# A shorter input ring, ten more groups of the spectrum kept on chip, and a new order of transfers between two stages

## The reference

```python
coeff = complex(xi[..., 0], xi[..., 1]) * sqrt_eig
x = einsum('nlm,mlk->nkm', coeff, pct)           # Legendre sums, one product per order m
u = irfft(x, n=512, axis=-1, norm='forward')     # h: 64 x 256 x 512
h = u + attention(layernorm(u))                  # key = x K, tanh logits, band of 12, softmax
h = h + ffn(layernorm(h))                        # 7 layers, only rows that a mask selects
```

## Time and profile before

| what | us |
|---|---|
| median of three runs (range) | 1428.83 (1427.85 to 1432.66) |
| the profiled execution, its own time | 1430.64 |
| span of its trace | 1428.6 |
| last group of stage 1 scaled | 319.05 |
| SyncE's first issue of stage 2 | 325.27 |

### The profile page before, as it was taken

One profiled execution on the slowest core, in us unless ns is written; L12 is line 12 of the kernel. 1 busy time (PEld: TensorE's weight loads), 2 busy tenths in 40 slices (PEclk: granted clock), 3 DMA queues, 4 the chain that ended last, 5 costly groups with the idle time before them and its releaser, 6 DMA issues. The chain is left out here.

```text
span 1428.6 us, 30500 instructions
## 1 busy us (share of the span) xinstructions
PE 1334.1 (93%) x8813; PEld 1158.9 (81%) x8813; DVE 929.4 (65%) x2026; ACT 899.9 (63%) x1956; POOL 559.5 (39%) x1394
## 2 busy tenths in 40 slices
PE   4999778798999999999999999999999989999994
PEld 3778666588899999999999999999999989545551
DVE  1232222235777878878788887888878878767772
ACT  1223222234677777777777777777777777867772
POOL 0000000000355555555555555555555546732222
PEclk8999999999999999999999999999999999999997
DMA  8999999994653433434334343343434332100000
GB/s 346 424 425 424 425 425 425 425 376 146 192 130 92 94 79 96 86 83 90 79 98 85 82 86 82 99 83 83 85 82 100 82 93 59 50 12 9 9 4 5
DMA packets 88315, 219.69 MB, mean 154 GB/s; under 512 B 20784, under 2 KB 33724, under 8 KB 75900
## 3 DMA queue, kind: packets, MB, share of 16 engines
q1 hardware_dynamic: 78728, 190.33, 42.8%
q10 hardware_dynamic: 4164, 27.27, 4.5%
q0 software_dynamic: 5376, 1.52, 0.6%
HBM read 147.77 MB, written 72.68 MB: 154 GB/s over the span
## 5 line engine op out<-in xcount | busy, mean ns | idle before, releaser
L674 PE MATMUL ps_k<-sphi,Glo 128*128 128x256 f32 x1024 | 292.2, 285 | 0.0
L673 PE MATMUL ps_k<-splo,Ghi 128*128 128x256 f32 x1024 | 291.0, 284 | 0.0
L672 PE MATMUL ps_k<-sphi,Ghi 128*128 128x256 f32 x1024 | 288.6, 282 | 0.0
L261 PE MATMUL s1b<-pg,cg 128*128 128x256 f32 x1024 | 240.5, 393 | 48.0 <-DVE cg L231 46.8
L261 PEld LDWEIGHTS s1b<-pg,cg 128*128 128x128 f32 x1024 | 198.0, 196 | 93.0 <-issue 33.9
L231 DVE TENSOR_TENSOR cg<-xg,se 128x1024 f32<-128x1024 f32 x63 | 77.2, 1225 | 221.5 <-DMA pg<-in_pct_dram 211.0
L1442 POOL TENSOR_SCALAR ve<-var 128x2 f32<-128x2 f32 x64 | 13.9, 217 | 479.8 <-ACT squares L1049 479.7
L672 PEld LDWEIGHTS ps_k<-sphi,Ghi 128*128 128x128 f32 x1024 | 194.7, 190 | 2.4
L673 PEld LDWEIGHTS ps_k<-splo,Ghi 128*128 128x128 f32 x1024 | 193.1, 189 | 2.7
L674 PEld LDWEIGHTS ps_k<-sphi,Glo 128*128 128x128 f32 x1024 | 193.7, 189 | 0.0
L316 ACT COPY stage<-s1b 128x512 f32<-128x512 f32 x104 | 60.7, 585 | 169.5 <-PE s1b L261 165.2
(11 more groups left out here) (175 smaller groups left out, 3181.0 us busy)
## 6 DMA issues: line engine op xcount, KB each, us to landing
pg<-in_pct_dram SPq DMA_DIRECT2D x63, 1024.0 KB, 25.7
out_dram<-o SPq DMA_DIRECT2D x64, 512.0 KB, 2.8
xg<-in_xs_dram SPq DMA_DIRECT2D x63, 512.0 KB, 24.2
xt<-spec SPq DMA_DIRECT2D x60, 512.0 KB, 5.2
spec<-stage ACTq DMA_DIRECT2D x52, 512.0 KB, 8.1
rrow<-rs SPq DMA_DIRECT2D x64, 128.0 KB, 4.6
spec<-hold SPq DMA_DIRECT2D x12, 480.0 KB, 5.2
recs<-rec SPq DMA_DIRECT2D x16, 160.0 KB, 5.6
```

The lines of the kernel that those rows point to most:

```text
L261: last = nc.tensor.matmul(bank[at * PARTS + part][:, m % 2, :], cg[:, b % SETS, m * 2 + h, :], pg[:, b, m * 2 + h, :], start=(h == 0), sto ...
L672: nc.tensor.matmul(out_ap, whi, mhi, start=(j == 0), stop=False)
L673: nc.tensor.matmul(out_ap, whi, mlo, start=False, stop=False)
L674: last = nc.tensor.matmul(out_ap, wlo, mhi, start=False, stop=(j == n - 1))
```

## The change

The ring has 4 slots, not 8. 22 groups are kept on chip (`KEPT`): the last 12 in `hold` as before, and the ten before them in a new tensor `apart`, which lies over the places that stage 2 gives to `lg`, `pr`, `pThi`, `pTlo`, `h`, `h2` and `o` (`h` is moved for that). `apart` is stored to `spec` by ten transfers of 512 KB, which SyncE issues behind the last load. VectorE's first write of `h` and SyncE's loads of blocks 1 and 2 wait for them (`apart_stored`). Block 0's rows from `spec` (84 partitions) are loaded ahead of group 60; its rows from `apart` and `hold` are all issued by ScalarE. The eight constants `others` move from SyncE's queue to the start of ScalarE's. `LEAD` is 26, and the quarters of the side product stand further apart. In stage 2, block 3's load comes behind the first row of roots, and the stores of `hold` are spread two, two and two pairs over slots 0 to 2, where one pair stood ahead of the slots and two, two, one in them.

```diff
-RING1 = 8
+RING1 = 4
-LEAD = 20
+LEAD = 26
 HELD = 12
+APART = 10
+KEPT = HELD + APART
+FIRST_KEPT = P - KEPT * GM // 2
+APART_AT = 179968
+        self.apart = nc.alloc_sbuf_tensor_at("apart", [P, APART * GM, NLAT], F32, offset=APART_AT)
-        KF_AFTER = {3: 0, 5: 1, 7: 2, 9: 3}
-        G_AFTER = {11: 0, 13: 1, 15: 2, 17: 3}
-        GLO_AFTER = {14: 0, 16: 1, 18: 2, 19: 3}
+        KF_AFTER = {3: 0, 6: 1, 9: 2, 12: 3}
+        G_AFTER = {15: 0, 18: 1, 21: 2, 23: 3}
+        GLO_AFTER = {17: 0, 20: 1, 23: 2, 25: 3}
+        def first_apart(eng, c):
+            eng.dma_start(const.x0[FIRST_KEPT:FROM, 2 * c:2 * c + 2, :].rearrange("p q w -> p (q w)"),
+                          const.apart[c * NB:c * NB + 1, :, :].rearrange("o (p q) w -> o p (q w)", q=2)
+                          ).then_inc(const.x0_loaded, 16)
...
@@ stage 1, SyncE
-                    for dst, src in ((Kf, K_in), (FT, FT_in), *others):
+                    for dst, src in ((Kf, K_in), (FT, FT_in)):
+            for half in range(2):
+                sp.wait_ge(stored[half], 32 * ((GROUPS - KEPT + 2 - 2 * half) // 4))
+            sp.dma_start(const.x0[0:FIRST_KEPT].rearrange("p (h q) w -> p h (q w)", h=2),
+                         spec[0].rearrange("(h p q) w -> p h (q w)", h=2, q=2)[0:FIRST_KEPT]
+                         ).then_inc(const.x0_loaded, 16)
             for g in range(GROUPS - RING1, GROUPS):
...
-            for half in range(2):
-                sp.wait_ge(stored[half], 32 * ((GROUPS - HELD) // 4))
-            sp.dma_start(const.x0[0:FROM] ...
-            for m0, m1 in (...): first_held(sp, c, m0, m1)
+            sp.wait_ge(copied, (GROUPS - HELD) * PARTS)
+            m_apart = NLAT - KEPT * GM
+            for j in range(APART * GM // 8):
+                for c in range(2):
+                    sp.dma_start(spec[0:NB, c * NLAT + m_apart + 8 * j:c * NLAT + m_apart + 8 * j + 8, :],
+                                 const.apart[c * NB:c * NB + NB, 8 * j:8 * j + 8, :]).then_inc(const.apart_stored, 16)
@@ stage 1, TensorE
-                    pe.wait_ge(copied, LEAD * PARTS)
+                    pe.wait_ge(copied, (LEAD - 2) * PARTS)
@@ stage 1, ScalarE
+                    if held and g < GROUPS - HELD:
+                        at_m = (g - GROUPS + KEPT) * GM + 2 * j
+                        to = const.apart[:, at_m:at_m + 2, :]
+                if isinstance(g, int) and g in (GROUPS - 8, GROUPS - 6):
+                    act.wait_ge(copied, (GROUPS - HELD) * PARTS)
+                    first_apart(act, (g - GROUPS + 8) // 2)
+                if isinstance(g, int) and g >= GROUPS - 3:
...
+                    for c in range(2):
+                        first_held(act, c, m0, m1)
+            for dst, src in others:
+                act.dma_start(dst, src).then_inc(const_loaded, 16)
             groups(nc.scalar, group)
-            first_held(act, 1, (HELD - 1) * GM, HELD * GM)
@@ stage 2, SyncE
-            for n in range(1, 4):
+            sp.wait_ge(const.apart_stored, 16 * APART * GM // 4)
+            for n in range(1, 3):
+                load_first(n, FROM)
-            store_held(0, 1)
+                if isinstance(i, int) and i == 0:
+                    load_first(3, FROM)
                 if isinstance(i, int) and 0 <= i < 3:
-                    store_held(1 + 2 * i, min(3 + 2 * i, 6))
+                    store_held(2 * i, 2 * i + 2)
@@ stage 2, VectorE, ahead of writing h
+                    if isinstance(n, int) and n == 0:
+                        dve.wait_ge(const.apart_stored, 16 * APART * GM // 4)
```

More of the change, by code:

```diff
@@ L88, in __init__ @@
         self.hold = sb("hold", [P, HELD * GM, NLAT])
+        self.apart_stored = ctx.enter_context(nc.semaphore("apart_stored"))
+        self.apart = nc.alloc_sbuf_tensor_at("apart", [P, APART * GM, NLAT], F32, offset=APART_AT)
     def add_ffn(self, nc, ctx):
@@ L161, in groups @@
                 group(g, g % RING1)
-            with eng.Fori(LEAD, GROUPS - HELD - RING1 + 1, RING1) as g0:
+            with eng.Fori(LEAD, GROUPS - KEPT - RING1 + 1, RING1) as g0:
                 for u in range(RING1):
                     group(g0 + u, (LEAD + u) % RING1)
-            for g in range(GROUPS - HELD, GROUPS):
+            for g in range(GROUPS - KEPT, GROUPS):
                 group(g, g % RING1)
@@ L297, in group @@
                 first, lead = isinstance(g, int) and g == 0, isinstance(g, int) and g < LEAD
-                held = isinstance(g, int) and g >= GROUPS - HELD
+                held = isinstance(g, int) and g >= GROUPS - KEPT
                 at = g % 3 if lead else b % SETS
@@ L311, in group @@
                         nc.scalar.copy(const.dc[:, :], bank[0][0:NB, 0, :])
-                    if held:
+                    if held and g < GROUPS - HELD:
+                        at_m = (g - GROUPS + KEPT) * GM + 2 * j
+                        to = const.apart[:, at_m:at_m + 2, :]
+                    elif held:
                         to = hold[:, (g - GROUPS + HELD) * GM + 2 * j:(g - GROUPS + HELD) * GM + 2 * j + 2, :]
@@ L334, in group @@
                     nc.scalar.copy(const.Ghi[:, c], side(c)).then_inc(act_Ghi, 1)
+            for dst, src in others:
+                act.dma_start(dst, src).then_inc(const_loaded, 16)
             groups(nc.scalar, group)
-            act.wait_ge(copied, GROUPS * PARTS)
-            first_held(act, 1, (HELD - 1) * GM, HELD * GM)
             for half in range(2):
-                act.wait_ge(stored[half], 32 * ((GROUPS - HELD) // 4))
+                act.wait_ge(stored[half], 32 * ((GROUPS - KEPT + 2 - 2 * half) // 4))
 def stage2_blocks(nc, const, ffn_consts, spec, recs, rs, out):
@@ L539, in wait_spectrum @@
             if isinstance(n, int) and n == 0:
-                eng.wait_ge(const.x0_loaded, 16 * 7)
+                eng.wait_ge(const.x0_loaded, 16 * 9)
             elif k == 0:
@@ L585, in load, with load_first @@
                              spec[n].rearrange("(h p q) w -> p h (q w)", h=2, q=2)).then_inc(x_loaded[k], 16)
-            for n in range(1, 4):
-                sp.dma_start(xt[0:FROM, n].rearrange("p (h q) w -> p h (q w)", h=2),
-                             spec[n].rearrange("(h p q) w -> p h (q w)", h=2, q=2)[0:FROM]).then_inc(x_loaded[n], 16)
+            def load_first(n, rows):
+                sp.dma_start(xt[0:rows, n].rearrange("p (h q) w -> p h (q w)", h=2),
+                             spec[n].rearrange("(h p q) w -> p h (q w)", h=2, q=2)[0:rows]).then_inc(x_loaded[n], 16)
                 for c in range(2):
```

6 lines of the change are left out of this document (5 added, 1 removed).

## The result

The changed kernel takes 1426.56 us, median of 20 runs; the kernel before took 1429.75 us on the same chip. The ratio is 0.9975, with a 95% interval of 0.9966 to 0.9983: 3.6 us less by the ratio (the two medians are 3.2 us apart), just under the 0.3% bound of the prediction, but clear of zero. Forecast were 8.0 us. The profiled execution took 1427.68 us.

A forecast was written before the change was run, and what follows sets the result against it. Transfers bound stage 1, and SyncE's chain was late entering stage 2. Stage 1: -12.4 + 0.8 - 2.1 = -13.7 us; plus 5.7 handed back, -8.0 us, so 1422.0 us; range 1417 to 1426, or to 1429 with (b) and most of (c).

The forecast's parts named there:

- the end of stage 1: Last scaling to h of block 0: ScalarE's issues hidden, 1.2 us if uncovered; `apart_stored` full at 332.3, h 1.1 us later.
- rival (c): Behind the last load: `apart`'s stores go slower, 20 us instead of 13.3; -1.3 us, 1429, the same; chance 0.08.
- A second term: End of stage 1: block 0's rows from DRAM, 0.34 MB issued before load 60, put 0.8 us in front of the last load.
- A third: Stage 2, behind `rrow` 2: four stores instead of two before the end of the `hold_stored` wait, 2 x 1.4 us more.
- the pace of 3.70 us a group from group 42 on: Late stage 1: groups with nothing stored take 3.70 us each; that stretch becomes ten groups longer.
- the ring at nothing: Stage 1: four slots need 11.2 us of a 14.8 us loop where nothing is stored, so the smaller ring costs nothing.
- The hole: Stage 1, 18 to 24 us, DMA at 249 GB/s: moving constants to ScalarE's queue closes it and saves 2.1 us.
- The chain at the start of stage 2: SyncE's rows of roots out and back, with `hold` stores between: `lsc` 0 to 3 move +0.9, +2.8, +2.8, +5.7 us.
- rival (a): Start of stage 2: rows return faster, stores drain at 12.4 us; 2.2 us handed back, -11.5 us, 1419; chance 0.14.
- my sign: Stage 2: if waits for `rrow` shrink instead of growing, the forecast's share handed back is wrong.
- rival (e): End of stage 1: removed transfers were not what ended it, or are paid in full after it; 0 to -3 us; chance 0.06.
- rival (b): Late stage 1: ring of four runs dry at times, 22 groups at 3.9 us; -3.6 us, 1427, the same; chance 0.13.

The follow-up runs named there:

- the kernel without `apart`: Kernel before plus ring of four, constants on ScalarE's queue and stage 2's new order, with 12 groups kept: ratio 0.9976 to before.
- the six early stores: Changed kernel with six groups in `apart` instead of ten, 92 rows from DRAM still in front: ratio 1.0001 to before.
- one kernel with ScalarE issuing and ten stores behind it: Changed kernel with block 0's rows from DRAM behind the last load, split into 80 and 4: ratio 0.9955 to before.
- with GpSimd: Changed kernel with DRAM rows behind the last load and seven of eight row transfers from `apart` and `hold` issued by GpSimd: ratio 0.9953 to before.

## Why the prediction was wrong, step by step

**The step that failed** is the one on the end of stage 1. I had ScalarE's issues as "hidden by what follows, and is worth 1.2 us if that cover goes", with `apart_stored` as the last thing that stage 2 waits for and nothing but the bytes in front of it. Up to h of block 0 I gave away 2.3 us; 7.6 were lost, 5.3 more. I had priced the rows by their issue. What they cost is their landing behind 5.24 MB of stores. Three things make up the 7.6 us:
- The rows of block 0 land behind `apart`'s stores: from the end of ScalarE's last issue to the cast there are 5.1 us for 0.7, so 4.4. Shown by putting the stores behind (wait of 2.33 us), by the kernel without `apart` (2.07) and by the six early stores (2.33). The engines are not full in that time: the share is 0.25 from 318 to 320 us and 0.04 from 320 to 322 us. The rows wait for a few engines that finish late. The Trainium skill, DMA: Bandwidth & Descriptors, section Queues, rings and completion order, says that a DMA engine's semaphore increment lands only after every earlier write of that engine, across its queues. By it rows on ScalarE's queue must wait for stores on SyncE's; the rows above agree, but small rows queued in turn behind the stores on each engine would look alike, and no run tells the two apart.
- ScalarE issues between its copies, with 1.0 to 1.5 us an issue: 2.1 us in this trace, 1.1 in the second trace of the same kernel. That copies wait for issues is seen in the rows (313.09 behind 313.04); the size is not a fixed price, since one kernel with ScalarE issuing and ten stores behind it lost nothing here.
- The last pair of issues instead of one, 0.6 us (1.97 for 1.39), as forecast. The rest, 0.4 us, lies between cast and h. There TensorE's granted clock is 0.50 from 316 to 324 us, the lower of its two levels (1.2 GHz), after it stood idle for 4.5 us; in before it is 0.55 to 0.60 from 326 to 330 us, so little of the loss is the clock's.

So `apart_stored` at 321.41 instead of 318.6 did not decide. Less the 2.4 us by which stage 1 ran later it is right to 0.4 us: the stores' own price was well sized, and rival (c) falls for this place. Moved to stage 2 they do run at 300 GB/s.

**A second term was too small:** block 0's rows from DRAM in front of load 60, "0.8 us more". They cost 4.0 us in the change, 1.5 of which stay when the rows are late. I took them by bytes at 425 GB/s, but at full share the engines moved 278 beside them. Of these 3.2 us too little, 1.0 came back at the last half group, which the same rows had stretched in before (2.9 us between its scalings for 1.8): I had counted the rows as a new cost only. This is in the main the 2.4 us by which the last scaling missed 305.4.

**A third was small too:** two more stores ahead of `hold_stored`, 2.8 us forecast, 3.7 measured (6.6 us of lead at `rrow` 2, 2.9 behind the wait), and 4.4 in the second trace (361.35 and 371.89).

**Right** were the pace of 3.70 us a group from group 42 on and the ring at nothing in the changed kernel. The hole closed as said, but that it saves 2.1 us at the end of stage 1 is not shown: alone it gave 0.45 us there, and together with the ring, in the kernel without `apart`, 0.8. The chain at the start of stage 2 came out better than I said: `rs` 0 landed in 2.6 us where I took 4.5, and `rrow` 0 to 1 took 14.3 us for 15.4. That is rival (a)'s first half, 3 us which hid part of the loss. It also spoiled my sign: the waits for `rrow` of blocks 0 and 1 shrank (3.28 to 1.40 us, 2.47 to 2.23), which I had said would mean too large a share handed back. The share was too small, because the loss lay ahead of this chain.

The outcome is rival (e) by its mechanism, to which I gave 0.06: the transfers removed did end stage 1, but are paid behind it, in full as far as the times can tell. The change with them (0.9975) and without them (0.9976) takes the same time. That 3.6 us is also the number of rival (b), and that 1426.56 lies between 1417 and 1429, is luck: the groups at the end never went at 3.9 us.

**What stays open:** why rows of DRAM slow the loads beside them; why moving the constants alone gains 5.3 us by time and 2.4 in the trace, more than the whole change by its point value (the intervals overlap); why the ring alone moves 402 GB/s up to 120 us; why the block ends late with GpSimd; and why groups 59 to 61 still lose 1.5 us when the rows are late. For the last there is a candidate. With GpSimd issuing, `apart`'s two pieces went out at 264.77, and these three groups lost 0.5 us (285.20 to 296.79) while the period from 266.24 took 4.24 us; but no run moves those pieces alone with the rows late. The kernel without `apart` has its rows late too, but as 104 in one piece. Against its 0.9976 (0.996 to 0.9992) the eight versions with `apart` and late rows stand at 0.9942 to 0.9989, five of them at 0.9957 or less, and only the first has its interval clear of it. So `apart` may be worth up to 0.3% once it is placed better; that is not shown, and an even split was not run without it.

The two lowest ratios are those of the change with its DRAM rows behind the last load, 0.9942 (0.993 to 0.9954), and of six groups, evenly split, with the old order of stage 2, 0.9950 (0.9932 to 0.9969). Both beat the kernel before. Only the first has an interval clear of the change's (0.9966 to 0.9983), and theirs overlap, so neither is shown to be the better.

## What to carry to other kernels

A transfer taken out from in front of the last load is saved only if what follows can start without it: here the stores moved behind that load, and the first small rows of the next stage landed behind the stores. Price a small transfer by what is in flight when it is issued, not by its bytes, and look at its number of rows before you put it in front of anything: 92 rows in one piece cost 0.3% against 80 and 12 (the intervals just touch). Undo a bundle part by part: one moved line, the constants', timed no slower alone than the whole bundle. And take a second trace of the same kernel before a difference of one or two microseconds is given a cause.

## What the runs showed of the hardware

- 0.34 MB read from DRAM in rows, beside loads of 0.5 and 1 MB, lowered the rate from 425 to 278 GB/s at a full share of 1.03; a full share does not say that bytes move.
- Stores of 512 KB moved with the last loads at 420 GB/s, and with nothing else queued by SyncE, at the head of stage 2, at 300 GB/s with a share of 0.99.
- Two issues, of 40 KB pieces first and 4 KB pieces then, held ScalarE for 2.98, 2.56 and 1.97 us while ten stores were queued by SyncE (2.18, 2.51 and 1.84 in the second trace), and for 1.48, 1.25 and 1.16 us with the stores put behind. So the length of an issue is a sign of what is in flight.
